# Six layers of windowed attention and feed-forward: the next layer's feed-forward input weights split in three pieces over three units

## The chip, the cores and the metric

The kernel runs on one core of one Trainium2 chip. The time is device microseconds of one execution; several executions are made and their median is given.

## The reference, cut to what matters

The input has 8 sequences of 256 tokens with 128 channels. A first attention layer is followed by six layers, each of a windowed attention (16 heads of 64, window 32) and a gated feed-forward with 341 hidden channels:

```
def ffn_layer(x, g, bln, W1, b1, W2, b2):
    mu = x.mean(-1, keepdims=True)
    var = ((x - mu) ** 2).mean(-1, keepdims=True)
    xn = (x - mu) / jnp.sqrt(var + 1e-05) * g + bln
    hg = xn @ W1 + b1                      # W1 is 128 x 682
    a, gate = jnp.split(hg, 2, -1)
    return a * jax.nn.gelu(gate, approximate=False) @ W2 + b2
for i in range(DEPTH):                     # DEPTH = 6
    x = attn_layer(shift_tokens(x), Wqkv[i], q_scale[i], k_scale[i], Wo[i]) + x
    x = ffn_layer(shift_tokens(x), ln_g[i], ln_b[i], W1[i], b1[i], W2[i], b2[i]) + x
```

## The kernel before, in words

After a setup (the first attention layer and the folding of the weights) the six layers run as one software pipeline over 48 units; unit n is sequence n % 8 of layer n // 8. All is written out by hand: every engine has a function `step(m, s)` that lists its calls in a fixed order, and `pipeline` calls it for each s from -1 to 49. In step s the name `after` is unit s + 1, `u` is unit s, `before` is unit s - 1 and `last` is unit s - 2. The attention's projections are made for `u`, its scores and values for `before`, and the feed-forward for `last`. Engines meet at semaphores alone, and each engine takes its instructions in the order of its list.

Products in the projections and in the first feed-forward matmul are made with operands split in a high part (rounded to the format that TensorE takes at full rate) and a low part, the rest. For W1 the parts are `w1_hi` and `w1_lo`, both with two buffers, for even and odd layers. ScalarE makes the high part by a copy (L1763), GpSimd the low part by a subtraction (L1388). In the profile's names `w1_s` is `w_s`, the parts are `w_hi` and `w_lo`, and `x2_hi`, `x2_lo` are `x_hi`, `x_lo`. The split of layer 0 is made in unit 0, and that of layer k in unit 8(k-1) + 5: `split_layer`. Both follow the splits of the normalised activations: `feed_hi` on ScalarE, `feed_lo` on GpSimd.

The raw weights `w1_s` have one buffer. SyncE's queue loads them for the next layer (`load_w1`, L1268). That queue also carries the copies of the values into the layout of the windows, `copy_v`: 14 transfers for the first token tile of a unit and 16 for the second, each behind a wait for ScalarE's last copy `copy_u(n, t, 3)` of that tile. Its order within a layer:

```
for i in range(2, 7):
    for t in range(TT):
        copy_v(layer * B + i, t)
    if i == 4:
        load_w1(layer + 1)
```

The calls near the change, in the order of each engine's step:

- ScalarE: `copy_o(last, 1)`, `copy_qkT(before, 1, 1, 1)`, `copy_u(u, 0, 0)`, `residual_hi(last)` (L1728, writes x_hi), `copy_u(u, 0, 1)`, `copy_u(u, 0, 2)`, `copy_u(u, 1, 0)`, `copy_center(last)`, `square_x(last)`.
- VectorE: `feed_1(last)` (L1526), `soft_scale(before, 0)`, `residual_lo(last)` (L1534, needs x_hi), `soft_top(before, 1)`, `soft_shift(before, 1)`, `feed_3(last)` (L1541, writes vtok).
- TensorE: `proj(u, 0, 5)`, `scores(before, 1)`, `proj(u, 0, 6)`, `proj(u, 1, 4)`, `feed_mean(last)` (needs x_lo). The projections use two banks in turn: `proj(u, 1, 4)` writes the bank that `proj(u, 0, 5)` wrote, and waits for `copy_u(u, 0, 1)`.
- GpSimd: `turn(u, 0, 1, 0)`, `turn(u, 0, 1, 1)`, `feed_rstd(last)` (L1375, waits for vtok), `normalise(u, 0, 1)`, two more turns, `feed_lo(last)`.

Of the kernel before, what the change touches and what calls it, by code (L numbers as in the profile page):

```python
# [26 lines left out]
ALU = mybir.AluOpType  # L27
# [6 lines left out]
B = 8  # L34
# [15 lines left out]
L = 6  # L50
# [7 lines left out]
DI = int(C * 4 * 2 / 3)  # L58
PIECES = [(0, 128), (128, 128), (256, DI - 256)]
UNITS = L * B  # L60
BANKS = 8
QK_BANKS = 4
HALF = 512
# [25 lines left out]
def build(nc, x, w_heads, bq_heads, bk_heads, w_v, b_v_rows, w_proj, b_proj_rows, wqk, q_scale_rows, k_scale_rows, wvt, wo,  # L89
          feed_cols, w1, w2, rope, ident, win_mask, win_pick, causal, positions, slope_heads, one_row, weights, out):  # L90
    with ExitStack() as ctx:
# [3 lines left out]
        def signal(name, per=1, start=0):  # L95
            return Signal(ctx.enter_context(nc.semaphore(name)), per, start)
# [97 lines left out]
        xh_a = signal("xh_a")  # L194
        xgh_a = signal("xgh_a")
        xgl_g = signal("xgl_g")
        w1h_a = signal("w1h_a")
        w1l_g = signal("w1l_g")
        w1_p = signal("w1_p", 3)
        gelu_a = signal("gelu_a", 3)  # L200
        hid_d = signal("hid_d", 3)
# [1018 lines left out]

            return FB if n < UNITS - 1 or i == 0 else SO[0] + i - 1

        def split_layer(n):

            return 0 if n == 0 else n // B + 1 if n % B == 5 and n // B < L - 1 else None

        def live(u):

            n = index(u)
            return not isinstance(n, int) or 0 <= n < UNITS  # L1230

# [6 lines left out]
        with nc.Block() as block:  # L1238
            @block.sync
            def _(sp):  # L1240
# [23 lines left out]
                    load_weights(sp, at, j)  # L1264

                def load_w1(layer):
                    sp.wait_ge(w1l_g.sem, w1l_g.at(layer - 1))
                    sp.dma_start(w1_s[:, :], w1[bass.ds(layer, 1), :, :].rearrange("o p n -> p (o n)")).then_inc(w1_in.sem, 16)  # L1268

                def load_w2(layer):  # L1270
# [48 lines left out]
            def _(pool):  # L1319
# [57 lines left out]
                def feed_lo(u):  # L1377
                    if not live(u):
                        return
                    n = index(u)  # L1380
                    pool.wait_ge(xgh_a.sem, xgh_a.at(n))
                    G.tensor_tensor(xg_lo[:, :], xg[:, :], xg_hi[:, :], ALU.subtract).then_inc(xgl_g.sem, 1)
                    layer = split_layer(n)
                    if layer is not None:
                        pool.wait_ge(w1h_a.sem, w1h_a.at(layer))
                        if layer >= 2:
                            pool.wait_ge(w1_p.sem, w1_p.at((layer - 1) * B - 1, 2))
                        G.tensor_tensor(w1_lo[:, layer % 2, :], w1_s[:, :], w1_hi[:, layer % 2, :], ALU.subtract).then_inc(w1l_g.sem, 1)  # L1388

                def normalise(u, t, kind):  # L1390
                    if not live(u) or begun(u, t):
# [7 lines left out]
                def step(m, s):  # L1399
# [26 lines left out]
                    normalise(u, 0, 0)  # L1426
                    turn(u, 0, 1, 0)
                    turn(u, 0, 1, 1)
                    feed_rstd(last)
                    normalise(u, 0, 1)  # L1430
                    turn(u, 1, 0, 0)
# [192 lines left out]
            def _(act):  # L1624
# [127 lines left out]
                def feed_hi(u):  # L1752
                    if not live(u):
                        return
                    n = index(u)
                    act.wait_ge(xh_a.sem, xh_a.at(n))
                    S.activation(xg_hi[:, :], xg[:, :], ACT.Copy).then_inc(xgh_a.sem, 1)
                    layer = split_layer(n)
                    if layer is not None:
                        act.wait_ge(w1_in.sem, 16 * layer + 16)  # L1760
                        if layer >= 2:
                            act.wait_ge(w1_p.sem, w1_p.at((layer - 1) * B - 1, 2))
                        S.activation(w1_hi[:, layer % 2, :], w1_s[:, :], ACT.Copy).then_inc(w1h_a.sem, 1)  # L1763

                def gelu(u, i):
                    if not live(u):
# [14 lines left out]
                def step(m, s):  # L1781
# [13 lines left out]
                        finish_copy(1)  # L1795
                    copy_qkT(before, 1, 1, 1)
                    copy_u(u, 0, 0)
                    residual_hi(last)
                    copy_u(u, 0, 1)
                    copy_u(u, 0, 2)  # L1800
# [42 lines left out]
            def _(pe):  # L1843
# [160 lines left out]
                def feed_w1(u, i):  # L2004
# [3 lines left out]
                    at, rows = PIECES[i]  # L2008
                    if i == 0:
                        if n % B == 0:  # L2010
                            pe.wait_ge(w1l_g.sem, w1l_g.at(n // B))
                        pe.wait_ge(xgl_g.sem, xgl_g.at(n))
                    elif n < UNITS - 1:
                        pe.wait_ge(hid_d.sem, hid_d.at(n, i - 1))
# [196 lines left out]
```

## Time and profile before

| | |
|---|---|
| median of 3 runs | 1687.85 us (1687.73 to 1692.02) |
| the profiled execution's own time | 1687.07 us |
| its span in the trace | 1685.0 us |
| TensorE busy, of the span | 96% |
| VectorE | 88% |
| ScalarE | 79% |
| GpSimd | 79% |

The busy shares are of one profiled execution. A busy TensorE is not one at its peak, since matmuls overlap. The pipeline of the 48 units takes the time from about 230 us on; the setup lies before.

### The profile page before, as it was taken

To read this page: it belongs to the slowest core of one execution; us is meant where nothing else is said; L and a number is where in the kernel's file an instruction comes from. 1 tells how busy PE (TensorE), PEld (TensorE's weight loads), DVE (VectorE), ACT (ScalarE), POOL (GpSimd) and SP (SyncE) were. 2 spreads that over 40 slices of the span, in tenths; PEclk is the share of its full clock that TensorE was granted. 3 is DMA by queue.
4 is the path that set the end of the run, shared out by engine and by line. 5 is a ranking of instruction groups with operands and counts; after the bars stand their busy time and mean duration, and the time that the engine had idled before them with its cause. 6 is when DMAs were issued, how large, how long until landed. Compare 5 with 4: busy or idle time off the path is not lost.

```text
span 1685.0 us, 70654 instructions
## 1 busy us (share of the span) xinstructions
PE 1621.3 (96%) x29226; PEld 1413.8 (84%) x29226; DVE 1482.9 (88%) x2314; ACT 1327.3 (79%) x2789; POOL 1334.1 (79%) x1798
## 2 busy tenths in 40 slices
PE   7999869999999999999999999999999999999997
PEld 5777547888888888898888989898898988988886
DVE  6887749999999999899999999999999999999984
ACT  6888737878878787887878788787888878888874
POOL 7777558888888888888888888888888888888870
PEclk9999989999999999999999999999999999999999
DMA  4588507566865656857567665658566667656654
GB/s 125 177 285 319 206 15 160 119 151 139 232 153 123 154 123 150 231 130 160 118 157 202 160 145 134 148 127 242 125 151 140 138 152 211 151 128 144 142 130 111
DMA packets 101407, 265.78 MB, mean 158 GB/s; under 512 B 26720, under 2 KB 34912, under 8 KB 101088
## 3 DMA queue, kind: packets, MB, share of 16 engines
q1 hardware_dynamic: 101088, 261.26, 61.5%
q8 instruction: 232, 3.80, 1.0%
q14 instruction: 87, 0.71, 0.1%
HBM read 45.15 MB, written 27.26 MB: 43 GB/s over the span
## 4 chain that ended last, share of the span: by engine, by line
PE 74%; POOL 5%; issue 3%; ACT 2%; SPq 1%; DVE 1%; DMA 0%; POOLq 0%; ACTq 0%; DVEq 0%
PE ps L1902 15%; PE ps L1893 15%; PE ps L1961 9%; PE ps L1917 9%; PE ps L1939 7%; PE ps L1949 4%; PE ps L2031 3%; PE ps L2020 2%; PE ps L2018 2%; PE ps L2019 2%; PE ps L1931 2%; POOL rot L1339 2%; POOL rot L1397 1%; SPq L1255 1%; PE ps L1992 1%
## 5 line engine op out<-in xcount | busy, mean ns | idle before, releaser
L1339 POOL TENSOR_TENSOR rot<-rot 128x512 f32<-128x512 f32 x380 | 492.0, 1311 | 50.7 <-DVE rot L1474 50.6
L1474 DVE TENSOR_TENSOR rot<-ps,rope_l 128x1024 f32<-128x1024 f32 x380 | 463.1, 1220 | 29.4 <-ACT sq L1638 17.6
L1397 POOL TENSOR_TENSOR rot<-rot,rnorm 128x1024 f32<-128x1024 f32 x190 | 362.2, 1906 | 17.7 <-POOL rnorm L1367 0.4
L1902 PE MATMUL ps<-w_t,xs_hi 128*128 128x256 f32 x1476 | 303.4, 298 | 13.2 <-PEq L374 11.0
L1648 ACT ACTIVATE un<-ps 128x512 f32<-128x512 f32 x384 | 229.5, 598 | 99.3 <-PE ps L1902 49.4
L1893 PE MATMUL ps<-w_t,xs_hi 128*128 128x512 f32 x784 | 262.9, 416 | 1.8 <-DVE rot L1474 1.7
L1638 ACT ACTIVATE sq<-ps 128x512 f32<-128x512 f32 x380 | 227.6, 599 | 45.2 <-PE ps L1893 24.5
L1902 PEld LDWEIGHTS ps<-w_t,xs_hi 128*128 128x128 f32 x1476 | 224.9, 189 | 27.8 <-issue 20.3
L1460 DVE TENSOR_REDUCE ssum<-sq 128x16 f32<-128x1024 f32 x190 | 230.1, 1211 | 12.3 <-ACT sq L1638 12.3
L1917 PE MATMUL ps<-ident_s,rot 128*128 128x128 f32 x1536 | 233.2, 274 | 6.0 <-ACT kT L1664 4.1
L1917 PEld LDWEIGHTS ps<-ident_s,rot 128*128 128x128 f32 x1536 | 180.5, 140 | 38.2 <-issue 15.4
L1902 PE MATMUL ps<-w_t,xs_lo 128*128 128x256 f32 x738 | 207.0, 280 | 0.0
L1961 PE MATMUL ps<-vk,pT 128*32 128x128 f32 (+1 forms) x6528 | 187.8, 268 | 0.6 <-ACT pT L1681 0.6
L1961 PEld LDWEIGHTS ps<-vk,pT 128*32 128x32 f32 x6528 | 162.1, 110 | 16.6 <-issue 15.7
L1893 PE MATMUL ps<-w_t,xs_lo 128*128 128x512 f32 x389 | 154.5, 397 | 0.0
L1939 PEld LDWEIGHTS ps<-kT,qT 64*32 64x32 f32 x12288 | 144.8, 105 | 6.5 <-issue 0.7
L1939 PE MATMUL ps<-kT,qT 64*32 64x64 f32 x12288 | 147.6, 224 | 0.1
L1893 PEld LDWEIGHTS ps<-w_t,xs_hi 128*128 128x128 f32 x784 | 123.7, 190 | 27.5 <-DVE rot L1474 10.4
L1902 PEld LDWEIGHTS ps<-w_t,xs_lo 128*128 128x128 f32 x738 | 139.0, 188 | 0.0
L1518 DVE TENSOR_TENSOR prob<-ps,linv 128x1024 f32<-128x1024 f32 x96 | 117.6, 1225 | 3.1
L1502 DVE TENSOR_REDUCE lsum<-ps 128x16 f32<-128x1024 f32 x96 | 116.7, 1215 | 2.7 <-ACT ps L1672 2.7
L1494 DVE TENSOR_TENSOR prob<-ps,smax 128x1024 f32<-128x1024 f32 x96 | 117.1, 1220 | 1.7
(158 smaller groups left out, 3533.1 us busy)
## 6 DMA issues: line engine op xcount, KB each, us to landing
vk<-un SPq DMA_DIRECT2D x1440, 128.0 KB
w_t<-weights_dram SPq DMA_DIRECT2D x48, 512.0 KB, 6.7
weights_dram<-rot SPq DMA_DIRECT2D x12, 1024.0 KB, 5.1
weights_dram<-sq SPq DMA_DIRECT2D x24, 512.0 KB, 3.6
raw<-wqk_dram SPq DMA_DIRECT2D x24, 256.0 KB, 4.5
wvt_s<-wvt_dram SPq DMA_DIRECT2D x12, 256.0 KB, 5.2
wo_s<-wo_dram SPq DMA_DIRECT2D x12, 256.0 KB, 5.5
w_s<-w_dram SPq DMA_DIRECT2D x6, 341.0 KB, 4.3
```

Source lines behind the costliest of these rows:

```text
L1339: last = G.tensor_tensor(cos[:, :, s, :], cos[:, :, s, :], sin[:, :, 1 - s, :], ALU.add)
L1397: G.tensor_tensor(v, v, rnorm[:, t, kind * H:(kind + 1) * H, None].broadcast_to([P, H, D]), ALU.mult).then_inc(nrm_g.sem, 1)
L1460: V.tensor_reduce(ssum[:, t, kind * H:(kind + 1) * H], sq[:, kind, :].rearrange("p (h e) -> p h e", h=H), AX_X, ALU.add).then_inc(ss_d.sem, 1)
L1474: V.tensor_tensor(dst, src[:, None, :, :].broadcast_to([P, 2, H // 2, D]), tab[:, :, None, :].broadcast_to([P, 2, H // 2, D]), ALU.mult).t ...
L1518: V.tensor_tensor(pairs, tile_scores(t).rearrange("p (hp a) k -> p hp a k", hp=2), inv, ALU.mult).then_inc(pn_d.sem, 1)
L1638: S.activation(sq[:, kind, half * 512:(half + 1) * 512], ps[:, PJ + PJ_BANK[t][2 * kind + half], :], ACT.Square).then_inc(sq_a.sem, 1)
L1648: S.activation(un[:, (u[1] % 2) * TT + t, j // 2, (j % 2) * HALF:(j % 2 + 1) * HALF], ps[:, PJ + PJ_BANK[t][QK_BANKS + j], :], ACT.Copy).t ...
L1893: last = M.matmul(bank, v, w_t[:, j, w, :], start=i == 0, stop=i == 2)
L1902: last = M.matmul(bank[:, cols], v, w_t[:, j, w, cols], start=i == 0, stop=i == 2)
L1917: last = M.transpose(ps[:, TP, a * P:(a + 1) * P], rot[:, kind, 0, c * P:(c + 1) * P], ident_s[:, :])
L1939: last = M.matmul(out_s, qT[rows, par, a, 32 * w:32 * w + 32], kT[rows, a, 32 * w:32 * w + 64], start=False, stop=a == PAIRS - 1)
L1961: last = M.matmul(ps[32 * k:32 * k + 32, SO[t], cols], pT[:, a, 32 * k:32 * k + 32], vk[:, 4 * t + k, a, cols], start=a == 0, stop=a == PA ...
```

## The change

The split of the next layer's W1 is cut in three pieces of 228, 228 and 226 columns. The pieces of layer k are made in units 8(k-1) + 3, + 4 and + 5, one in each; those of layer 0 are all made in unit 0. On ScalarE they stand ahead of `residual_hi(last)`, on GpSimd ahead of `feed_rstd(last)`; before, the whole split stood behind the activations' splits. The wait for the load (`w1_in`), and that for the last reader of the buffer, move with the pieces. SyncE's order is as it was, but for the count that `load_w1` waits for, and TensorE waits for the third piece.

```
+W1_PIECE = 228
...
-        w1h_a = signal("w1h_a")
-        w1l_g = signal("w1l_g")
+        w1h_a = signal("w1h_a", 3)
+        w1l_g = signal("w1l_g", 3)
...
+        def w1_pieces(n):
+
+            if n == 0:
+                return [(0, i) for i in range(3)]
+            return [(n // B + 1, n % B - 3)] if n % B in (3, 4, 5) and n // B < L - 1 else []
...
                 def load_w1(layer):
-                    sp.wait_ge(w1l_g.sem, w1l_g.at(layer - 1))
+                    sp.wait_ge(w1l_g.sem, w1l_g.at(layer - 1, 2))
...
+                def feed_w1_lo(u):
+                    if not live(u):
+                        return
+                    for layer, i in w1_pieces(index(u)):
+                        pool.wait_ge(w1h_a.sem, w1h_a.at(layer, i))
                         if layer >= 2:
                             pool.wait_ge(w1_p.sem, w1_p.at((layer - 1) * B - 1, 2))
-                        G.tensor_tensor(w1_lo[:, layer % 2, :], w1_s[:, :], w1_hi[:, layer % 2, :], ALU.subtract).then_inc(w1l_g.sem, 1)
+                        at = w1_cols(i)
+                        G.tensor_tensor(w1_lo[:, layer % 2, at], w1_s[:, at], w1_hi[:, layer % 2, at], ALU.subtract).then_inc(w1l_g.sem, 1)
...
                     turn(u, 0, 1, 1)
+                    feed_w1_lo(last)
                     feed_rstd(last)
...
+                def feed_w1_hi(u):
+                    if not live(u):
+                        return
+                    for layer, i in w1_pieces(index(u)):
                         act.wait_ge(w1_in.sem, 16 * layer + 16)
                         if layer >= 2:
                             act.wait_ge(w1_p.sem, w1_p.at((layer - 1) * B - 1, 2))
-                        S.activation(w1_hi[:, layer % 2, :], w1_s[:, :], ACT.Copy).then_inc(w1h_a.sem, 1)
+                        at = w1_cols(i)
+                        S.activation(w1_hi[:, layer % 2, at], w1_s[:, at], ACT.Copy).then_inc(w1h_a.sem, 1)
...
                     copy_u(u, 0, 0)
+                    feed_w1_hi(last)
                     residual_hi(last)
...
                         if n % B == 0:
-                            pe.wait_ge(w1l_g.sem, w1l_g.at(n // B))
+                            pe.wait_ge(w1l_g.sem, w1l_g.at(n // B, 2))
```

## Rows read from the trace of the kernel before

**Rows 1.** The page: busy time of each engine, and the granted clock in 40 slices.

```profile
PE 1621.3 (96%) x29226; PEld 1413.8 (84%) x29226; DVE 1482.9 (88%) x2314; ACT 1327.3 (79%) x2789; POOL 1334.1 (79%) x1798
...
PEclk9999989999999999999999999999999999999999
```

**Rows 2.** One line's instructions, both W1 splits (durations in ns, starts).

```profile
L1763 ACT ACTIVATE w_hi<-w_s x6: 755/757/758, 296.7 to 1390.5; 128x682 fp32r<-128x682 f32 x6
L1388 POOL TENSOR_TENSOR w_lo<-w_s,w_hi x6: 1390/1515/1651, 297.6 to 1391.3; 128x682 fp32r<-128x682 f32 x6
```

**Rows 3.** SyncE's queue around the first load (start, duration, line).

```profile
364.65 1.89 SPq L1255 DMA_DIRECT2D vk<-un  x3
...
385.35 0.59 SPq L1268 DMA_DIRECT2D w_s<-w_dram  x1
```

**Rows 4.** The line of the load: five issues, and the time until they land.

```profile
L1268 SPq DMA_DIRECT2D w_s<-w_dram x5: 582/585/590, 385.3 to 1330.6; - x5
DMA to landing us min/median/max: 4.0/4.2/4.5
```

**Rows 5.** ScalarE's timeline, unit 4's last copy of tile 0 and around unit 3's x_hi.

```profile
363.98 0.60 ACT L1648 ACTIVATE un<-ps 128x512 f32<-128x512 f32 x1 [0.23 <-PE ps L1902]
...
376.20 0.42 ACT L1728 ACTIVATE x_hi<-xT 128x256 fp32r<-128x256 f32 x1 [1.31 <-DVE xT L1526]
376.53 0.58 ACT L1648 ACTIVATE un<-ps 128x512 f32<-128x512 f32 x1
```

**Rows 6.** The same x_hi and the same load in three later layers.

```profile
612.41 0.42 ACT L1728 ACTIVATE x_hi<-xT 128x256 fp32r<-128x256 f32 x1 [1.31 <-DVE xT L1526]
621.74 0.59 SPq L1268 DMA_DIRECT2D w_s<-w_dram  x1
1085.17 0.42 ACT L1728 ACTIVATE x_hi<-xT 128x256 fp32r<-128x256 f32 x1 [1.31 <-DVE xT L1526]
1094.87 0.58 SPq L1268 DMA_DIRECT2D w_s<-w_dram  x1
1321.55 0.42 ACT L1728 ACTIVATE x_hi<-xT 128x256 fp32r<-128x256 f32 x1 [1.31 <-DVE xT L1526]
1330.60 0.58 SPq L1268 DMA_DIRECT2D w_s<-w_dram  x1
```

**Rows 7.** TensorE's timeline: proj(u, 1, 4), feed_mean, and the two projections behind them.

```profile
377.71 0.63 PE L1893 MATMUL ps<-w_t,xs_hi 128*128 128x512 f32 x2
...
378.41 0.28 PE L1982 MATMUL ps<-x_hi,center 128*128 128x256 f32 x1
...
378.65 0.66 PE L1893 MATMUL ps<-w_t,xs_hi 128*128 128x512 f32 x2
...
379.38 0.62 PE L1893 MATMUL ps<-w_t,xs_hi 128*128 128x512 f32 x2
```

**Rows 8.** Windows ahead of the pipeline: busy time and count per engine, clock, DMA.

```profile
218.99:222.00 3.01, 0.00 (x0) 0.00 (x0) 1.68 (x2) 1.08 (x3) 1.37 (x6) 0.98 0.00 0
222.00:229.97 7.97, 0.00 (x1) 0.03 (x1) 0.17 (x1) 0.26 (x1) 6.81 (x7) 0.50 0.00 0
229.97:235.30 5.33, 5.33 (x19) 4.68 (x20) 0.06 (x1) 1.95 (x4) 0.64 (x1) 0.50 0.00 0
```

**Rows 9.** TensorE's timeline at half clock: two projections in succession.

```profile
232.67 1.05 PE L1893 MATMUL ps<-w_t,xs_hi 128*128 128x512 f32 x2
...
233.95 1.05 PE L1893 MATMUL ps<-w_t,xs_hi 128*128 128x512 f32 x2
```

**Rows 10.** GpSimd's timeline: the wait ahead of L1375 in unit 0 and unit 5.

```profile
291.75 0.72 POOL L1375 TENSOR_TENSOR rtok<-vtok,minus_half 128x2 f32<-128x2 f32 x1 [0.65 <-DVE vtok L1541]
439.87 0.72 POOL L1375 TENSOR_TENSOR rtok<-vtok,minus_half 128x2 f32<-128x2 f32 x1 [1.02 <-DVE vtok L1541]
```

**Rows 11.** Who TensorE waited for from 250 to 1640 us (total, times, longest).

```profile
PE ps L1917 <- ACT kT L1664: 3.2, 6, 0.5
...
PE ps L1931 <- ACT o L1691: 2.4, 5, 0.6
```

More of the change, by code:

```diff
@@ L1221, in feed_bank, with w1_cols @@
             return FB if n < UNITS - 1 or i == 0 else SO[0] + i - 1
-        def split_layer(n):
-            return 0 if n == 0 else n // B + 1 if n % B == 5 and n // B < L - 1 else None
+        def w1_pieces(n):
+            if n == 0:
+                return [(0, i) for i in range(3)]
+            return [(n // B + 1, n % B - 3)] if n % B in (3, 4, 5) and n // B < L - 1 else []
+        def w1_cols(i):
+            return slice(i * W1_PIECE, min((i + 1) * W1_PIECE, 2 * DI))
         def live(u):
@@ L1382, in feed_lo @@
                     G.tensor_tensor(xg_lo[:, :], xg[:, :], xg_hi[:, :], ALU.subtract).then_inc(xgl_g.sem, 1)
-                    layer = split_layer(n)
-                    if layer is not None:
-                        pool.wait_ge(w1h_a.sem, w1h_a.at(layer))
+                def feed_w1_lo(u):
[3 more added lines that the diff above has]
+                        pool.wait_ge(w1h_a.sem, w1h_a.at(layer, i))
                         if layer >= 2:
                             pool.wait_ge(w1_p.sem, w1_p.at((layer - 1) * B - 1, 2))
-                        G.tensor_tensor(w1_lo[:, layer % 2, :], w1_s[:, :], w1_hi[:, layer % 2, :], ALU.subtract).then_inc(w1l_g.sem, 1)
+                        at = w1_cols(i)
+                        G.tensor_tensor(w1_lo[:, layer % 2, at], w1_s[:, at], w1_hi[:, layer % 2, at], ALU.subtract).then_inc(w1l_g.sem, 1)
                 def normalise(u, t, kind):
@@ L1757, in feed_hi @@
                     S.activation(xg_hi[:, :], xg[:, :], ACT.Copy).then_inc(xgh_a.sem, 1)
-                    layer = split_layer(n)
-                    if layer is not None:
+                def feed_w1_hi(u):
+                    if not live(u):
+                        return
+                    for layer, i in w1_pieces(index(u)):
                         act.wait_ge(w1_in.sem, 16 * layer + 16)
```

## The prediction

> **What bounds the kernel now.** I read the page first: TensorE is busy 96% of the span, VectorE 88%, the other two 79%, and the granted clock stands at full speed in all slices of the pipeline [rows 1]. Then TensorE's timeline: in a unit of some 29.5 us its instructions follow one another with hardly a gap. The table of who waited for whom names few waits of TensorE for another engine. Two are of interest: L1917 waited for ScalarE's kT copy 6 times, and L1931 for ScalarE's copy of o 5 times [rows 11]. These are the units in which W1 is split. So TensorE sets the pace. A microsecond that it loses anywhere is lost at the end, and a microsecond that another engine saves is worth something only where TensorE waited for it.
>
> Last I read the queue of SyncE, since a wait for a load is moved, and the reader should do that for every moved wait: find the time at which the new place comes up, and the time at which what it waits for is there.
>
> **The old place.** The split is six ScalarE copies of 757 ns and six GpSimd subtractions of 1.39 to 1.65 us [rows 2]. Behind them TensorE waits 3.2 us and 2.4 us in all [rows 11]. For the six units that is 0.53 us each on the kT copy, and 0.48 us each on the copy of o in five units. In the units 8(k-1) + 5 this gives 5 x 0.53 + 2.4 = 5.1 us, which I count as gain in full; if TensorE makes the waits good later by being behind anyway, it is nothing.
>
> **The new place, and the load.** Unit 3 of a layer gets the first piece. On ScalarE it stands right ahead of x_hi, and waits for the load of the next layer's W1. In unit 3, x_hi starts at 376.20 us [rows 5]. The load is issued at 385.35 us [rows 3], 9.15 us later. It lands 4.0 to 4.5 us after its issue, 4.2 in the middle [rows 4]. In the last layer that loads, the issue is at 1330.60 us [rows 6] and the split, in the old place, at 1390.5 us [rows 2], 55 us behind the landing: that is why the trace shows no wait for it.
>
> Could the load come earlier in the new kernel? It stands in SyncE's queue behind unit 4's 30 copies. The first of them is issued at 364.65 us [rows 3], when ScalarE has done unit 4's last copy of the first tile (363.98 + 0.60 us) [rows 5]. From there to the load are 20.7 us for 30 issues. Nothing that the change touches lies ahead of this: the copies, their waits and their order stay, and the count that the load itself waits for was reached in the layer before. So the load keeps its time relative to unit 4's copies, which are all made before ScalarE comes to the new wait. There is no deadlock in it, only a wait.
>
> The gap between x_hi and the issue of the load is 9.15 us in the first layer, then 9.33, 9.70 and 9.05 us in those shown [rows 3, 5, 6]; the pair that is not shown has 9.14 us. The sum is 46.4 us. Five landings of 4.2 us add 21.0 us. Then the piece itself: the copy behind a 256-column copy starts 0.33 us later [rows 5], so a piece of 228 columns moves x_hi by some 0.31 us, with 0.03 us to wake, 0.34 us; five of them are 1.7 us. x_hi comes 46.4 + 21.0 + 1.7 = 69.1 us later over the five layers, some 13.8 us each time.
>
> **Who is behind the waiting instruction.** On ScalarE x_hi and, behind it, `copy_u(u, 0, 1)`. On VectorE `residual_lo` needs x_hi, so that VectorE stands too, with all that follows it. TensorE can do `proj(u, 0, 5)`, `scores(before, 1)` and `proj(u, 0, 6)`, as before, and then stands at `proj(u, 1, 4)`, whose bank `copy_u(u, 0, 1)` has to free. That copy starts 0.33 us after x_hi and takes 0.58 us [rows 5], so with 0.04 us to wake TensorE could go 0.95 us after x_hi. In the kernel before it went at 377.71 us, 1.51 us after it [rows 5, 7]. So it has 0.56 us of slack, 2.8 us over five layers, and loses 69.1 - 2.8 = 66.3 us. `feed_mean` comes 0.70 us behind the start of that projection [rows 7], when VectorE has made x_lo (some 0.5 us behind the end of x_hi), so it adds nothing. I see no place where the loss is made good: TensorE has no idle time in a unit to give.
>
> **The clock.** TensorE stands for some 12.8 us in each of the five places. The trace has one such gap: no matmul from 218.99 to 229.97 us. The granted clock fell to half (1.2 GHz) about 3 us into it, and stayed there for the first 5.33 us of dense work after it, with TensorE busy throughout [rows 8]. Two projections then start 1.28 us apart [rows 9], against 0.73 us at 2.4 GHz [rows 7], a factor of 1.75. So 5.33 us at half clock did the work of 3.04 us, and cost 2.3 us. Five times that is 11.5 us. The lower bound is nothing, if the clock does not fall or the other engines set the pace at that moment; the upper is twice, 23 us. I take the row, since gap and work are alike. The Trainium skill ("TensorE: Matmul & The Clock Gate", Part 1) says that idleness throttles the array's clock and that in a model "the ramp penalty is <1% of a typical kernel span"; by that the term would be anything from nothing up to 16.9 us, and could be dropped, where the trace's gap gives 11.5.
>
> **The other pieces.** In units 4 and 5 the load has landed long ago. ScalarE idled 1.31 us ahead of x_hi [rows 5], so a piece of 0.31 us is covered. On GpSimd a piece of 228 columns costs some 0.7 us by the rates of the 682-column rows (1.39 us and 1.65 us, less than in proportion) [rows 2]; GpSimd waits 1.02 us there for vtok, so it is covered too, by 0.3 us [rows 10]. In unit 0 all three stand there, 2.1 us against a wait of 0.65 us [rows 10]: 1.4 us of delay for the inverse root and all behind it, against the 1.4 to 1.6 us and TensorE's 0.5 us on kT taken off later in the unit. I count nothing, plus or minus 1 us. Without their cover the ten pieces on either engine would cost 3 us on ScalarE and 7 us on GpSimd.
>
> **Sum.** 66.3 + 11.5 - 5.1 = 72.7 us on the profiled execution's 1687.07 us (its span is 1685.0, 2.1 us lie around it) gives 1759.8 us. The median of the runs shown is 0.8 us above that execution, so 1760.6 us: I say 1761.
>
> **Rivals.**
>
> 1. The clock costs nothing: it stays up or, after the stop, the chain mean, variance, inverse root on the other engines sets the pace. Then 66.3 - 5.1 = 61.2 us, 1749 us. For it: the chain has little slack, and GpSimd waits for vtok in each unit. Against: at half clock TensorE was busy 5.33 of 5.33 us [rows 8]. Chance 0.10. The rule of the Trainium skill named above, taken as leave to drop the term, ends here too.
>
> 2. The stop costs more than its length: the half clock lasts twice as long, or the engines come out of step and need a unit to recover, 2 us more each. Then 1760.6 + 11.5 = 1772 us or more. For it: the trace shows one gap alone, ahead of a pipeline that was still filling. Chance 0.09.
>
> 3. No stop at all, and the change does what it says. One mechanism: the load has landed when unit 3's slot comes up. That needs a landing by 376.2 us where the trace has 385.35 + 4.2 = 389.6; it is decided by SyncE's 30 copies, which would have to end 13.4 us sooner. Then only the gain of 5.1 us is left, 1683 us (faster, by 0.3%), or 1687 us, if TensorE doesn't use it. For it: only an error of mine in which unit stands in that slot. Against: the last split, unit 37's, starts at 1390.5 us [rows 2], 68.9 us after the x_hi at 1321.55 us [rows 6]. The first split, unit 0's, starts 10.4 us after its own x_hi (286.3 us, at the same line); so 58.5 us, two units, lie between, and the x_hi that I read is unit 35's, the third after a layer's first. Chance 0.04.
>
> The forecast has 0.77. By this the kernel is slower with 0.96; a measurement of this kernel can tell some 0.3%, 5 us, from no change. Of rival 3's 0.04 I give half to faster and half to the same. The range runs from rival 1 with a gain of 2 us more (1747 us) to rival 2's 1773 us.
>
> **What the new profile should show.** ScalarE's first piece in units 3, 11, 19, 27 and 35 waits for the DMA of w_s, some 15 us each and 75 us in all. TensorE has no matmul for 12.5 to 13.5 us there, and the granted clock is at half from within these gaps to about 5 us behind them. VectorE stands as well. The waits of L1917 for kT and of L1931 for o are gone. The intervals from x_hi to x_hi of the other units are as before, 29.0 to 29.7 us, the one behind unit 5 some 1 us shorter than its 30.4 us. Wrong it is if the piece in unit 3 starts without a wait for the DMA, if the load is issued at another distance behind unit 4's copies, or if TensorE, having lost 13 us, needs less time for what follows.

## The result and the profile after

The changed kernel takes 1757.66 us (median of 4 runs, 1753.96 to 1760.68) against 1687.8 us of the kernel before on the same chip: a ratio of 1.0406, 95% interval 1.0385 to 1.0428. It is slower by 70 us; 73 had been forecast. The execution that was profiled took 1753.96 us, 66.9 more than the one profiled before.

The page of the changed kernel: span, busy time, TensorE's busy share in 40 slices of 43.8 us, the chain's shares, and the transfers of instructions (count, MB).

```profile
span 1752.2 us, 70694 instructions
...
PE 1633.7 (93%) x29226; PEld 1423.5 (81%) x29226; DVE 1484.2 (85%) x2314; ACT 1328.8 (76%) x2801; POOL 1331.8 (76%) x1810
...
PE   7999779979999979999979999799999799999997
...
PE 73%; SPq 7%; issue 2%; POOL 1%; DMA 1%; ACT 1%; DVE 1%; POOLq 0%; ACTq 0%; DVEq 0%
...
q8 instruction: 232, 3.80, 1.0%
```

Against [rows 1] the engines' busy times hardly moved: the span grew and their shares fell. Only TensorE has 12 us more, part of it work at half clock. Its row of slices has a 7 in the 9th, 15th, 21st, 26th and 32nd, one for each layer but the last; before, all slices from the 7th to the 39th have a 9. "SPq" has 7% of the chain: work on other engines hung on the issues of SyncE. The waits of the whole span (waiting engine, tile and line, who released it: total us, times, longest):

```profile
ACT w_hi L1779 <- DMA w_s<-w_dram: 70.2, 5, 14.6
DVE x_lo L1546 <- ACT x_hi L1740: 61.7, 6, 12.8
PE ps L1910 <- ACT un L1660: 61.5, 5, 12.9
```

One wait, five times: ScalarE for the load of W1, and behind it VectorE and TensorE for ScalarE. The first of the five, on SyncE's queue and on ScalarE (start, duration, in brackets the idle time ahead and who ended it), then TensorE in front of and behind its stop:

```profile
361.79 20.95 SPq L1262 DMA_DIRECT2D vk<-un  x30
...
382.78 0.58 SPq L1275 DMA_DIRECT2D w_s<-w_dram  x1
```

```profile
371.42 0.60 ACT L1660 ACTIVATE un<-ps 128x512 f32<-128x512 f32 x1
...
385.89 0.39 ACT L1779 ACTIVATE w_hi<-w_s 128x228 fp32r<-128x228 f32 x1 [13.87 <-DMA w_s<-w_dram]
386.19 0.40 ACT L1740 ACTIVATE x_hi<-xT 128x256 fp32r<-128x256 f32 x1
```

```profile
373.95 0.74 PE L1910 MATMUL ps<-w_t,xs_hi 128*128 128x512 f32 x2
...
387.12 1.22 PE L1910 MATMUL ps<-w_t,xs_hi 128*128 128x512 f32 x2 [12.20 <-ACT un L1660]
```

ScalarE comes to the piece at 372.02 us, SyncE is in the middle of its 30 copies, and the load goes out at 382.78, 20.99 us behind the first copy, where [rows 3] have 20.7. The piece starts 3.1 us after the issue. The load's own line says the same of all five:

```profile
L1275 SPq DMA_DIRECT2D w_s<-w_dram x5: 580/580/583, 382.8 to 1383.7; - x5
DMA to landing us min/median/max: 3.1/3.2/3.2
```

3.2 us in the middle, against 4.2 in [rows 4]. Windows of the first stop and of what follows it, then of the work behind the second (bounds, length, busy time and count of TensorE, its weight load, VectorE, ScalarE, GpSimd, then the granted clock, the DMA engines' share and GB/s):

```profile
375.00:376.80 1.80, 0.00 (x0) 0.00 (x0) 0.00 (x0) 0.00 (x0) 1.80 (x2) 0.98 0.85 191
376.80:387.12 10.32, 0.00 (x0) 0.00 (x0) 0.50 (x1) 1.23 (x4) 0.91 (x2) 0.50 0.74 176
387.12:390.30 3.18, 3.18 (x9) 2.60 (x10) 2.46 (x3) 1.58 (x4) 0.00 (x0) 0.50 0.00 0
390.30:393.00 2.70, 2.70 (x19) 2.33 (x18) 0.99 (x2) 1.86 (x4) 0.75 (x2) 0.99 0.00 0
...
636.50:642.80 6.30, 5.79 (x19) 4.81 (x19) 3.04 (x3) 3.55 (x8) 0.41 (x1) 0.50 0.00 0
```

The clock is at half (1.2 GHz) from within the stop until 3 to 6 us behind it; in the third window it comes back just after the window's end, at 390.38 us, and in the last one at 642.97 us. TensorE worked at half speed for 3.26, 5.95, 3.02, 2.95 and 5.67 us, 20.85 us in all; by the factor 1.75 of [rows 7, 9], 0.43 of that is loss, 8.9 us.

**Where the time went.** x_hi is written once in each unit, so its starts cut the pipeline in intervals. The table takes each interval less the same interval of the kernel before and sums this over the layers (us). A column's name gives the two units, by n % 8, whose x_hi bound the interval. All experiments are in it; each is explained further down.

| kernel | unit 2 to 3 (the stop) | 3 to 4 (behind it) | 5 to 6 | all others | ratio of times, 95% interval |
|---|---|---|---|---|---|
| after | 64.4 | 6.9 | -4.5 | 2.7 | 1.0406 (1.0385 to 1.0428) |
| e1_load_early | -0.8 | 0.0 | -2.0 | 5.4 | 0.9983 (0.9970 to 0.9996) |
| e3_units456 | 0.6 | 0.0 | -0.5 | 3.5 | 0.9991 (0.9980 to 1.0002) |
| e4_wait_alone | 63.3 | 6.3 | 0.6 | 1.8 | 1.0431 (1.0414 to 1.0447) |
| e6_whole_at_5 | -1.1 | -0.1 | -3.0 | 3.7 | 0.9993 (0.9981 to 1.0005) |
| e2_load_mid | 11.1 | 1.1 | -3.8 | 2.2 | 1.0054 (1.0037 to 1.0071) |
| e8_old_place | -0.8 | 24.9 | -0.9 | 6.4 | 1.0161 (1.0137 to 1.0185) |
| e5_warm | 69.8 | 0.1 | 8.9 | 7.2 | 1.0530 (1.0510 to 1.0550) |
| e7_warm_wide | 62.5 | 5.5 | 14.2 | 10.2 | 1.0516 (1.0492 to 1.0539) |
| e9_warm_256 | 69.1 | -0.6 | -3.2 | 3.5 | 1.0396 (1.0368 to 1.0425) |
| e10_tiny_48 | -1.4 | 5.7 | 13.3 | 12.1 | 1.0162 (1.0139 to 1.0186) |
| e11_tiny_256 | 0.9 | 21.0 | 1.2 | 7.3 | 1.0110 (1.0089 to 1.0131) |
| e12_early_shift | -4.3 | -0.7 | -2.3 | -8.6 | 0.9913 (0.9894 to 0.9933) |

For the changed kernel the four sum to 69.5 us (69.4 unrounded). The pipeline began 2.6 us earlier in this execution, because its setup was that much shorter, and the end has 0.4 us more: 67.2 us, the difference of the two spans. The first x_hi, the pipeline's mark, moves by such an amount with no edit near it, so it is taken as chance. The table sets single executions beside each other; entries of 2 or 3 us are within what such an execution moves by, and verdicts on small differences go by the ratios.

### The profile page after: what moved, and what is told of

The parts are those of the page before. It is cut to its first block, busy times and chain, and to the rows that moved or that the text cites. A ratio compares the mean times of both kernels' runs of the same rounds, so it can differ in the third digit from the quotient of the medians.

```text
span 1752.2 us, 70694 instructions
## 1 busy us (share of the span) xinstructions
PE 1633.7 (93%) x29226; PEld 1423.5 (81%) x29226; DVE 1484.2 (85%) x2314; ACT 1328.8 (76%) x2801; POOL 1331.8 (76%) x1810
## 4 chain that ended last, share of the span: by engine, by line
PE 73%; SPq 7%; issue 2%; POOL 1%; DMA 1%; ACT 1%; DVE 1%; POOLq 0%; ACTq 0%; DVEq 0%
PE ps L1910 16%; PE ps L1919 14%; PE ps L1978 9%; PE ps L1934 9%; SPq L1262 7%; PE ps L1956 7%; PE ps L1966 4%; PE ps L2048 3%; PE ps L2037 2%; PE ps L2035 2%; PE ps L2036 2%; PE ps L1948 2%; PE ps L2009 1%; DMA w_s<-w_dram 1%; PE ps L2018 1%
## 5 line engine op out<-in xcount | busy, mean ns | idle before, releaser
L1910 PE MATMUL ps<-w_t,xs_hi 128*128 128x512 f32 x784 | 268.8, 424 | 65.0 <-ACT un L1660 61.5
L1919 PE MATMUL ps<-w_t,xs_hi 128*128 128x256 f32 x1476 | 304.3, 298 | 13.7 <-PEq L375 11.0
L1919 PEld LDWEIGHTS ps<-w_t,xs_hi 128*128 128x128 f32 x1476 | 225.4, 190 | 28.9 <-issue 20.5
L1934 PE MATMUL ps<-ident_s,rot 128*128 128x128 f32 x1536 | 234.0, 275 | 2.5 <-POOL rot L1408 1.2
L1934 PEld LDWEIGHTS ps<-ident_s,rot 128*128 128x128 f32 x1536 | 181.4, 140 | 34.2 <-issue 12.4
L1919 PE MATMUL ps<-w_t,xs_lo 128*128 128x256 f32 x738 | 207.3, 281 | 0.0
L1910 PEld LDWEIGHTS ps<-w_t,xs_hi 128*128 128x128 f32 x784 | 126.7, 194 | 92.5 <-ACT un L1660 71.1
L1910 PE MATMUL ps<-w_t,xs_lo 128*128 128x512 f32 x389 | 157.1, 404 | 0.0
L1956 PEld LDWEIGHTS ps<-kT,qT 64*32 64x32 f32 x12288 | 146.5, 105 | 7.2 <-issue 1.1
L1956 PE MATMUL ps<-kT,qT 64*32 64x64 f32 x12288 | 149.5, 226 | 0.3 <-issue 0.3
L1919 PEld LDWEIGHTS ps<-w_t,xs_lo 128*128 128x128 f32 x738 | 139.3, 189 | 0.0
L1497 DVE TENSOR_REDUCE smax<-ps 128x16 f32<-128x1024 f32 x96 | 116.5, 1213 | 4.1 <-PE ps L1956 4.1
```

The costliest lines, as they stand in the source:

```text
L1910: last = M.matmul(bank, v, w_t[:, j, w, :], start=i == 0, stop=i == 2)
L1919: last = M.matmul(bank[:, cols], v, w_t[:, j, w, cols], start=i == 0, stop=i == 2)
L1934: last = M.transpose(ps[:, TP, a * P:(a + 1) * P], rot[:, kind, 0, c * P:(c + 1) * P], ident_s[:, :])
L1956: last = M.matmul(out_s, qT[rows, par, a, 32 * w:32 * w + 32], kT[rows, a, 32 * w:32 * w + 64], start=False, stop=a == PAIRS - 1)
```

## The experiments

### Is it the wait, and the wait alone?

Theory A: the loss is the wait for the load, which SyncE issues behind unit 4's copies. Rival B: part of it comes from the pieces themselves, three copies and three subtractions put ahead of x_hi and of the inverse root. e1 issues the load one unit sooner, e3 makes the pieces one unit later, and e4 is the kernel before with nothing but the wait ahead of x_hi.

```
e1, SyncE, on the kernel after
-                        if i == 4:
+                        if i == 3:
                             load_w1(layer + 1)
e3, on the kernel after
-            return [(n // B + 1, n % B - 3)] if n % B in (3, 4, 5) and n // B < L - 1 else []
+            return [(n // B + 1, n % B - 4)] if n % B in (4, 5, 6) and n // B < L - 1 else []
e4, ScalarE, residual_hi of the kernel before
+                    if n % B == 3 and n // B < L - 1:
+                        act.wait_ge(w1_in.sem, 16 * (n // B) + 32)
```

> The changed kernel, with the load of the next W1 issued one unit earlier in SyncE's queue (behind unit 3's copies in place of unit 4's). Theory (the stop is the wait for the load, nothing else): the load lands some 15 us before unit 3's slot, ScalarE doesn't wait, the granted clock stays at full speed in the whole pipeline, and what is left is the gain behind unit 5, 4 to 5 us: 1683 us, range 1681 to 1687. Rival (the pieces' place costs: three copies ahead of x_hi, three subtractions ahead of the inverse root): at most a few us of the 70 go away by another load, and the time stays above 1740 us.

> The changed kernel with the three pieces in units 4, 5 and 6 of a layer in place of 3, 4 and 5; the load stays where it is. Theory: unit 4's slot comes some 15 us behind the landing, no wait, and the time is that of the kernel with the early load, 1683 us (1681 to 1687). Rival (the pieces' place costs): above 1740 us. The two kernels of this pair reach the same state in two ways; if they differ by more than 2 us, the load's own traffic or the unit in which a piece stands matters.

> The kernel before, whole split in its old place in unit 5, with one thing added: in unit 3 ScalarE waits ahead of x_hi until the next layer's W1 has landed. Theory: the wait alone gives the whole loss, without the gain: what the changed kernel took and some 5 us more, 1763 us (1757 to 1768), with five waits of 14 us and the clock at half behind each. Rival (pieces and place cost a part): clearly below 1757 us.

Measured: e1 1687.38 us, e3 1687.13, e4 1760.76, against 1688.76. e1 and e3 are just above what was expected, since the gain of 4 to 5 us is only 1.5 to 3 us in them. The wait alone, with the split in its old place and whole, costs what the change costs; the pieces in their new place, with the load there in time, cost nothing. Rival B is out. ScalarE in e1 around the same piece, and the wait that e4 puts in:

```profile
373.86 0.39 ACT L1779 ACTIVATE w_hi<-w_s 128x228 fp32r<-128x228 f32 x1
...
375.27 0.42 ACT L1740 ACTIVATE x_hi<-xT 128x256 fp32r<-128x256 f32 x1 [1.03 <-DVE xT L1538]
```

```profile
ACT x_hi L1730 <- DMA w_s<-w_dram: 69.3, 5, 14.7
```

In e1 the piece has no idle time ahead of it, and ScalarE still idles 1.03 us for xT ahead of x_hi, where [rows 5] have 1.31: the piece lies in idle time, as the prediction had it. Which of two waits comes last can be read here: the load's is gone, the old one is back.

### How late may the load be?

e2 issues the load behind unit 4's first 14 copies. e8 leaves SyncE as it is and moves only the pieces back to the place of the old split, behind the activations' splits, still in units 3 to 5. e6, another question, makes all three pieces in unit 5 in the new place: what is the spreading worth?

```
e2, SyncE
                     for t in range(TT):
                         copy_v(layer * B + i, t)
-                    if i == 4:
-                        load_w1(layer + 1)
+                        if (i, t) == (4, 0):
+                            load_w1(layer + 1)
e8, GpSimd                      e8, ScalarE
-  feed_w1_lo(last)             -  feed_w1_hi(last)
   feed_rstd(last)                 residual_hi(last)
   ...                             ...
   feed_lo(last)                   feed_hi(last)
+  feed_w1_lo(last)             +  feed_w1_hi(last)
e6
-            return [(n // B + 1, n % B - 3)] if n % B in (3, 4, 5) and n // B < L - 1 else []
+            return [(n // B + 1, i) for i in range(3)] if n % B == 5 and n // B < L - 1 else []
```

> The changed kernel with the load issued between unit 4's 14 copies of the first tile and its 16 copies of the second: half the way to the early load. Theory (TensorE's loss is landing minus slot minus 0.6 us of slack, one for one): the load is issued at 373.5 to 374 us of the time of the kernel before and lands 3.2 to 4.2 us later, x_hi comes 1 to 2 us late, TensorE loses 0.4 to 1.5 us in each of five places and its clock doesn't fall: 2 to 8 us above the kernel with the early load, 1688 to 1695 us. Rival (a load close to the slot is as bad as a late one, or the slack is larger): above 1700 us, or no difference to the early load.

> The changed kernel's three pieces in units 3, 4 and 5, but behind the activations' splits, where the whole split stood, in place of ahead of x_hi; load as in the kernel before. Theory (slot against landing): unit 3's slot is now at 386.2 us of the time of the kernel before, the landing at 388.5 to 389.9 us, so ScalarE waits 2.3 to 3.6 us ahead of the kT copy in five places, TensorE loses 1.5 to 3.6 us in each, the clock doesn't fall, and the gain behind unit 5 is smaller, since a third of the split stays there: 1694 to 1704 us. Rival (any wait for the load in unit 3 throws the pipeline out of step): above 1720 us.

> The changed kernel with all three pieces in unit 5, at the new place (ahead of x_hi and ahead of the inverse root), and none in units 3 and 4; the load has long landed. It tells what spreading the pieces over units is worth, apart from the place. Theory: no stop; ScalarE's 0.95 us fit in its 1.3 us of idleness, GpSimd's 1.9 us exceed its 1.0 us by 0.9 us, which comes back as a wait of TensorE in unit 5 of each layer: 0.5 to 1 us five times, so 2 to 5 us above the kernel with the early load and about the time of the kernel before, 1686 to 1692 us. Rival (spreading is worth nothing): equal to the early load within 1 us.

Measured: e2 1696.65 us, e8 1717.37, e6 1687.03, against 1688.54. e6, e3 and e1 are alike within their intervals: spreading the split over three units is worth nothing that these runs can tell.

e2 lost more than expected. Its queue and the piece:

```profile
361.48 10.08 SPq L1262 DMA_DIRECT2D vk<-un  x14
371.60 0.58 SPq L1275 DMA_DIRECT2D w_s<-w_dram  x1
```

```profile
375.18 0.39 ACT L1779 ACTIVATE w_hi<-w_s 128x228 fp32r<-128x228 f32 x1 [3.47 <-DMA w_s<-w_dram]
```

The first 14 copies take 10.1 us, near half of 20.95, so the issue came about 1 us later than reckoned. ScalarE waits 3.5 us, of which its old idle time of 1.3 us covers a part; some 2.2 us a layer are left, 11.1 in the table. Another 1.1 us comes from the clock, which the expectation held up: TensorE stopped for 1.5 to 1.95 us in the five places, and behind two of these stops, of 1.81 and 1.58 us, the granted clock was at half for over 3 us. The intervals behind these two are 1.0 and 1.4 us longer than before, the other three 0.35 to 0.5 us shorter.

e8 missed by more. ScalarE waits here 2.9 to 4.1 us for the load, at a place behind x_hi. The expectation held the clock up in so short a stop. ScalarE, TensorE, and the windows of the first one:

```profile
390.20 0.39 ACT L1779 ACTIVATE w_hi<-w_s 128x228 fp32r<-128x228 f32 x1 [4.02 <-DMA w_s<-w_dram]
```

```profile
391.22 0.63 PE L1934 MATMUL ps<-ident_s,rot 128*128 128x128 f32 x4 [4.29 <-ACT kT L1676]
```

```profile
391.00:392.20 1.20, 0.98 (x9) 1.01 (x10) 0.24 (x1) 1.20 (x4) 0.55 (x2) 1.00 0.00 0
392.20:395.80 3.60, 3.60 (x125) 2.65 (x126) 3.17 (x5) 2.93 (x6) 2.77 (x9) 0.53 0.00 0
```

TensorE stopped for 4.29, 4.39, 3.21, 3.34 and 3.76 us, 19.0 us in all. In four of the five the granted clock fell to half. In the second one it did so within the stop, in the other three 1.0 to 1.5 us after TensorE had gone on. At half TensorE worked for 3.4, 5.1, 3.4 and 3.4 us, 15.3 us; times 0.43 that is 6.6 us. 19.0 + 6.6 = 25.6, and the table has 24.9. In the stop of 3.21 us the clock stayed. So here a third is added to the stop by the clock, where in the changed kernel 8.9 us come on 61.5.

### Is the term of the clock real, and can it be had back?

If TensorE worked through the stop, the clock should stay up and the interval behind it should lose nothing. e5 puts 100 transposes of the identity into a free bank ahead of the stopped projection, e7 twelve products of 512 columns. By the page's counts a transpose is two instructions and a wide product four: 200 and 48 added in each layer.

```
 proj(u, 0, 6)
+if 0 <= index(last) < UNITS - B and index(last) % B == 3:
+    keep_warm(100, TP)                                        # e5: 100 transposes
+    for _ in range(12):                                       # e7, in place of e5's line
+        M.matmul(ps[:, TP, :], ident_s[:, :], rope_l[:, 0:512], start=True, stop=True)
```

> The changed kernel, and in units 3, 11, 19, 27 and 35 TensorE runs 100 transposes of the identity into a bank that nobody reads, between proj(u, 0, 6) and proj(u, 1, 4), so that it is busy for some 11 us of the 12.2 us in which it stands. Nothing else is left out or added. Theory (the clock costs 2 to 3 us behind each stop): the granted clock stays at full speed, and the time falls by 8 to 13 us against the changed kernel, to 1745 to 1750 us, and the runs differ by less than 1 us. Rival (the clock costs nothing, other engines set the pace behind a stop): no change, 1754 to 1761 us as the changed kernel has it, or some us more if the transposes last longer than the wait.

> The changed kernel with TensorE kept busy in the five stops, as with the 100 transposes, but by 12 matmuls of 512 columns (32-bit, ident by a rotary table, into the bank that nobody reads at that point): 48 instructions in place of 200, for some 10.2 us of the 12.2 us. Theory (the 100 transposes did remove the clock's cost, 7 us, and what made that kernel slower, waits of TensorE for nothing that the profile shows ahead of dense small matmuls, came from the many instructions): these waits go, the clock stays up, the interval behind each stop is as in the kernel before, and the time is 4 to 9 us below the changed kernel, 1748 to 1754 us. Rival (keeping TensorE busy in a stop costs by itself, through the landing of the load or heat of the array): slower than the changed kernel again, above 1762 us.

Measured: e5 1779.69 us against 1688.76, e7 1776.62 against 1688.54; both slower than the changed kernel and far above the 1745 to 1754 us that were expected. In e5 most of the term of the clock is gone all the same: 0.1 us behind the stop, not 6.9. Four of the five intervals are 0.34 to 0.61 us shorter than before, and one is 2.2 us longer, where the clock was at half for over 3 us behind a rest of the stop of 2.58 us. In e7 the clock stayed up in two of the five alone: the rests of its stops, which the twelve products left open, were 1.2 to 2.05 us, and the three longest of them (1.94, 2.04, 2.05) were followed by half clock. Its 5.5 us in this column come from these and from a wait of the kind that follows. TensorE in e5, in the first stop and behind it:

```profile
377.47 11.08 PE L1882 MATMUL ps<-ident_s 128*128 128x128 f32 x100
...
390.44 0.73 PE L1910 MATMUL ps<-w_t,xs_hi 128*128 128x512 f32 x2 [1.89 <-ACT un L1660]
```

What was lost lies elsewhere, one and a half to nearly eight units behind the edit, under "issue": TensorE waited for nothing that the list of waits shows. Waits of e5, then of e7:

```profile
PE ps L1956 <- issue: 15.2, 9, 2.5
...
PE ps L1919 <- issue: 9.5, 5, 3.6
```

```profile
PE ps L1956 <- issue: 18.4, 14, 4.1
...
PE ps L1919 <- issue: 8.6, 4, 4.1
```

L1956 is the scores, L1919 the projections. The rival that many small instructions fill a queue falls: e7 adds 48 and loses as much as e5 with 200. What is left is that any number added moves all later instructions. The page of the changed kernel has a hint of it, in its line of queue 8: 232 transfers of instructions with 3.80 MB, 16.4 KB each. TensorE has 2 x 29,226 = 58,452 recorded instructions, 252 for each transfer. With 64 bytes for one (an estimate: 3.80 MB by 58,452 is 65) a transfer holds 256. If TensorE waits where such a block begins, then what counts is not how many instructions are added but where this puts the later blocks' bounds.

### Instruction blocks

Theory C: an addition of 256 leaves every later bound at the same instruction, and costs only its own time; one of 48 moves the bounds, and costs more although it is smaller. Rival D: cost goes with the count. e10 and e11 add small products (32 columns, two instructions each) to the kernel before, once in each layer but the last, where no stop is. e9 is e7 on the count of 256.

```
e10 and e11, on the kernel before; e9, on the kernel after, at the place of e5
+if 0 <= index(last) < UNITS - B and index(last) % B == 3:
+    for i in range(24):                 # e10; 128 in e11, 108 in e9; two instructions each
+        rows, k = slice(0, 64), i % 4
+        M.matmul(ps[32 * k:32 * k + 32, TP, 0:32], wpick[rows, 0, 32 * k:32 * k + 32], wmask[rows, 0, 0:32],
+                 start=True, stop=True)
+    for _ in range(10):                 # e9 alone: 40 more, 256 in all
+        M.matmul(ps[:, TP, :], ident_s[:, :], rope_l[:, 0:512], start=True, stop=True)
```

> The changed kernel with TensorE kept busy in the five stops by exactly 256 instructions: 108 small bf16 products (64x32, 32 columns) and 10 matmuls of 512 columns, each a weight load and a matmul, into the bank that nobody reads. The page gives 232 instruction transfers with 3.80 MB, 16.4 KB each, so 256 instructions of 64 bytes: TensorE's program comes in blocks of 256 instructions. Theory (in the two kernels with 100 transposes or 12 wide matmuls the clock's cost was gone, and the rest was added by the blocks' boundaries, which 200 or 48 further instructions per stop moved to other places of the unit): with 256 the boundaries stay where they were, TensorE's waits for nothing that the profile shows are as few as in the changed kernel (some 12 us on matmuls in place of 30), the clock stays up, and the time is 4 to 9 us below the changed kernel's ratio of 1.0406, that is 1.035 to 1.038, 1748 to 1753 us. Rival (keeping TensorE busy in a stop costs by itself): above 1.045, 1765 us or more.

> The kernel before, no stop in it, with 24 small bf16 products (48 instructions) added on TensorE in units 3, 11, 19, 27 and 35, behind proj(u, 0, 6), into a bank that nobody reads. By themselves they take some 0.6 us each time, 3 us in all. Theory (moved block boundaries cost): waits of TensorE for nothing that the profile shows, of 1 to 4 us each, ahead of the scores' small matmuls and the projections, as in the kernel with 12 wide matmuls; 10 to 25 us above the kernel before, 1698 to 1714 us. Rival (those waits came from the busy stops): 1690 to 1694 us.

> The same with 128 small products (256 instructions) in each of the five units: more than five times the added work, 3 us each time, 15 us in all, but the boundaries of blocks of 256 instructions stay. Theory: the waits for nothing that the profile shows are as in the kernel before; the time is what the products take themselves, 1696 to 1706 us, and no more than 5 us above, or below, the kernel with 48 instructions. Rival (each added instruction costs its fetch): above the kernel with 48 instructions by 12 us or more.

Measured, against 1690.96 us: e10 1718.65, e11 1711.02, e9 1759.73. All three are 5 to 7 us above the range that was expected under theory C. But a fifth of the instructions costs more, and the intervals of the two ratios are apart: D falls. Waits in e10, then in e11 (whose L2054 is the added work itself):

```profile
PE ps L1939 <- issue: 20.0, 14, 4.4
...
PE ps L1902 <- issue: 9.0, 4, 4.5
```

```profile
PE ps L2020 <- issue: 9.9, 18, 0.9
...
PE ps L2054 <- issue: 9.8, 5, 2.2
...
PE ps L2019 <- issue: 3.0, 5, 0.7
PE ps L1939 <- issue: 2.3, 3, 1.2
```

With 48 the waits ahead of scores and projections are 29.0 us. With 256 that ahead of the scores is 2.3 us, and the waits on W1's products (L2019, L2020) are 12.9 us, near the kernel before's 9.9:

```profile
PE ps L2020 <- issue: 7.5, 18, 0.8
...
PE ps L2019 <- issue: 2.4, 5, 0.7
```

In each added burst there is one such wait, 2 us each, 9.8 in all: 128 small products seem to run through faster than the next block comes. The transfers of queue 8 rise from 232 to 237 in e11, whose added instructions are 5 x 256, and to 236 in e5, with 1,000 added; the other queue that carries instructions stays at 87. (One more or less says nothing: e1, with nothing added, has 233.)

The trace also has the start of each transfer, and it ties the waits to them. In e10 TensorE waited 14 times for more than 1 us under "issue" from 300 to 1660 us. Each of these waits ends 2.3 to 2.9 us behind the start of a transfer of queue 8. In e5 it is 12 of 12, in e7 15 of 16, between 2.2 and 3.0 us. The transfers start 6.2 us apart in e10 (median), so by chance one wait in eight would end there. Here is the transfer ahead of e10's wait that ends at 1183.38 us, found in a window of 0.2 us, from 1180.90 to 1181.10 us:

```profile
q8 instruction: 1, 0.02, 29.7%
```

So TensorE waits for its next block.

e9 has the waits of e5 and e7 gone, and the clock up in the stop:

```profile
380.30:391.19 10.89, 8.82 (x27) 3.69 (x21) 0.50 (x1) 1.24 (x4) 0.59 (x1) 1.00 0.66 154
391.19:394.50 3.31, 3.31 (x11) 2.72 (x12) 2.46 (x3) 2.18 (x5) 0.00 (x0) 0.66 0.00 0
```

```profile
PE ps L1956 <- issue: 0.7, 2, 0.5
```

The intervals behind the stops sum to -0.6 us, 7.5 less than in the changed kernel, although behind the first of the five, shown here, the clock still fell, 1 us after TensorE had gone on behind a rest of the stop of 2.07 us; the other four are -0.33 to -0.49. So the clock's term is shown in the trace. In the time it is not: 1.0396 lies in the changed kernel's interval, since e9's stops are 4.7 us longer. Its copies are slower:

```profile
364.23 22.54 SPq L1262 DMA_DIRECT2D vk<-un  x30
```

22.54 us for the 30 in the first layer and 21.6 to 21.9 in the others, where the changed kernel has 20.7 to 21.6: 4.3 us more over the five. But e5 has 20.3 to 22.6, and e4, in which nothing of TensorE is changed, 20.3 to 21.7: they vary from layer to layer with no work added. What sets their pace is open.

### A version that beats both

If the bounds' places have a price, the kernel before pays one too: 9.9 us on W1's products. e12 is e1, with all bounds moved once by 240 instructions, put ahead of TensorE's first waits in the pipeline, when it has nothing else to do.

```
 pipeline, TensorE, ahead of its first step
+for i in range(120):
+    k = i % 4
+    M.matmul(ps[32 * k:32 * k + 32, TP, 0:32], wpick[0:64, 0, 32 * k:32 * k + 32], wmask[0:64, 0, 0:32],
+             start=True, stop=True)
```

> The kernel with the early load (ratio 0.9983 to the kernel before), and 120 small products (240 instructions) once, ahead of the pipeline, where TensorE waits for the last part of the setup for 11 us; their results are read by nobody. Nothing is added in the pipeline. It moves all boundaries of blocks of 256 instructions by 240, that is 16 back, which is where the kernel with 48 instructions per stop had them in its last full layer, units 36 to 42, seven intervals that were 2.1 us shorter than in the kernel before. Theory (the place of the boundaries sets TensorE's waits for nothing that the profile shows: 10 us on L2020 and L2019 of the kernel before): these waits get shorter, and the time falls by 5 to 12 us, 1676 to 1683 us; a ratio of 0.992 to 0.996. Rival (the shorter intervals of that layer were chance, or the products delay the start of the pipeline by as much): the ratio of the kernel with the early load, 0.998, or up to 1.002.

Measured: 1673.19 us (1667.70 to 1678.56) against 1687.8, ratio 0.9913 (0.9894 to 0.9933), 3 us below the expected range. All that TensorE waited for most, from 300 to 1640 us, first in e1 and then in e12:

```profile
PE ps L2037 <- issue: 8.4, 18, 0.9
...
PE ps L2036 <- issue: 3.2, 5, 1.0
```

```profile
PE ps L1914 <- issue: 3.5, 3, 2.1
PE ps L1938 <- POOL rot L1408: 1.0, 1, 1.0
```

(Lines stand 4 further down in e12.) The 11.6 us on L2036 and L2037 are gone from the list, whose top line is 3.5 us. By the ratios e12 is 0.70% ahead of e1, 12 us. The waits are most of it: from 300 to 1640 us TensorE is idle for 17.3 us in e1 and for 8.4 us in e12. What gave the rest is open. The Trainium skill ("Runtime: NRT & Kernel Launch", Instruction fetch mechanics) has instructions fetched in blocks of 256 in 16 KiB and the cost mostly hidden. The size agrees with 16.4 KB for a transfer; the hiding doesn't here, with 29 us of waits in e10 and 12 us gained between e1 and e12.

## Why the prediction was right, point by point

- **The old place.** [rows 11] promised 5.1 us. L1934's waits for kT and L1948's for o are gone from the list, and the interval behind unit 5 is 4.5 us shorter in all. But e1, with this gain and no stop, is only 0.17% faster, 2.9 us. From 300 to 1640 us its TensorE idles for 17.3 us, and that of the kernel before for 16.5: other waits have come in place of these. W1's products have 11.6 us in place of 9.9, and one projection of unit 5 starts late by "issue", with 1.5 us more lost behind it at half clock. This wait ends 1.4 us behind a transfer's start, so it is not of the kind above, and its cause is open:

```profile
453.20 0.70 PE L1910 MATMUL ps<-w_t,xs_hi 128*128 128x512 f32 x2 [1.95 <-issue]
```

- **The load's place in the queue.** Right: 20.99 us after the first copy, reckoned 20.7, and the count that it waits for, reached a layer before, adds nothing.
- **The landing.** 3.2 us in place of 4.2, five times: 5.2 us less by the five values. This is the larger mis-sized term: x_hi came 64.4 us later, for 69.1. It was taken from a time in which all engines run, and here the load is awaited by engines that stand, but this alone is not the reason. It was 3.0 to 3.3 us in all 25 landings that fell in a long stop (the changed kernel, e4, e5, e7, e9), also where TensorE was given work. But in e11, which has no such stop, TensorE was busy throughout the five landings and VectorE, ScalarE and GpSimd for 62% or more of each, and they took as little:

```profile
DMA to landing us min/median/max: 3.1/3.2/3.3
```

In e8, where ScalarE did nothing during the first landing and the others were busy for 18 to 35% of it, it took 3.95 us, and all five 3.9 to 4.6. e1 has both, 3.2 us twice and 4.0 to 4.2 three times. What decides it is open.
- **What stands behind ScalarE.** Right: TensorE stopped at L1910, `proj(u, 1, 4)`, for 61.5 us in five; 69.1 - 5.2 - 2.8 = 61.1. The slack that was reckoned as 0.56 us each shows as 0.33 to 0.49 in the interval behind the stop, where e9 has no clock to pay: 2 us, not 2.8.
- **The clock.** Right in kind, too large in size: 11.5 reckoned from one gap with 5.33 us at half behind it, 8.9 measured over five (2.95 to 5.95 us). The rest of the term held: the clock fell within the stop, 2 to 5 us into it, and TensorE was busy nearly throughout behind it. Rival 1, that the clock costs nothing, is out by e9 against the changed kernel, 7.5 us in the intervals behind the stops. The Trainium skill ("TensorE: Matmul & The Clock Gate", Part 1), with its bound of 1% for the ramp, agrees in size, 8.9 of 1752 us being 0.5%. The leave to drop the term, which the prediction weighed, doesn't hold here, since it is an eighth of the loss.
- **The other pieces at nothing.** Right: e3, e1 and e6.
- **The sum.** 64.4 (x_hi) - 2.0 (slack) + 8.9 (clock) - 4.5 (gain) + 2.7 (other intervals, reckoned as nothing) - 2.6 (setup, by chance) + 0.4 (end) = 67.3 us, for 72.7. The profiled execution was 66.9 us longer. The median of the four runs is 3.7 us above it, where before it was 0.8. So the forecast of 1761 us for 1757.66 is nearer than the terms deserve: the profiled execution was missed by 5.8 us, and half of that was made good by where the other runs happened to lie. The 30 copies are on the path five times; in the stopping kernels (the changed one, e4, e5, e7, e9) they take 20.2 to 22.6 us, which would be enough for it. This is argued, not shown: other runs than the profiled one have no trace.
- **Rival 2**, a stop that costs more than its length, has its sign wrong: the engines fell back into step at once, and the other intervals together have 2.7 us, no more than in e1, e3 and e6, which don't stop. **Rival 3**, no stop, is what e1 makes of the change: 1687.38 us, its second value.

## What to carry to other kernels

When a wait is moved up in an in-order queue, find two times before all else: when the new place comes up, and when what it awaits is there; the wait costs the difference, on every engine behind it, and issuing the load one unit sooner made it nothing. A short stop of TensorE is dear for its length: 3.2 to 4.4 us cost a third more through the clock, 12 us a seventh, and a stop need not be that long to pay (e2's of 1.6 and 1.8 us did). And in a kernel of tens of thousands of instructions look at the waits put down to "issue" at one and the same line: moving all of TensorE's instructions by a constant count, ahead of its first wait, was worth four times what the change's own idea was (12 us against 3).

## What the runs showed of the hardware that was not expected

- Instructions arrive in blocks, and TensorE can wait up to 4.5 us at a bound. In e10, 240 instructions beside TensorE's 58,452 lead to 29 us of such waits. One of the fourteen ahead of the scores:

```profile
1183.38 0.64 PE L1939 MATMUL ps<-kT,qT 64*32 64x64 f32 x21 [4.38 <-issue]
```

- The granted clock can fall after a short stop, up to 1.5 us after the work has resumed, and the length of the stop alone doesn't decide it. It fell in e2 after stops of 1.58 and 1.81 us and not after one of 1.95, and in e8 after stops of 3.34 to 4.39 us and not after one of 3.21.
- The same load of 341 KB lands in 3.0 to 3.3 us or in 3.9 to 4.8, and whether the engines work doesn't decide it (e11, e8 and e1 above).
- The 30 copies ahead of the load, alike in all kernels, take 19.8 to 23.4 us on their queue.
